# Keys and values of a fused transformer kernel: five evacuated blocks per sigmoid unit, value weights split in two loads, the down product's first operand tiles made before the values end

## The chip, the cores and the metric

The kernel runs as one launch on one core of a Trainium2 chip. The metric is device time in microseconds (us), lower is better. Before the change three runs took 1525.17 us in the median (1520.86 to 1525.78). The engines in this text: PE (TensorE, matmul), ACT (ScalarE), DVE (VectorE), POOL (GpSimd, which here issues loads and takes maxima over partitions), SP (SyncE, which here issues stores and loads).

## The reference

A model of two layers on 4096 tokens of width 256: cross-attention with mask, a feed-forward layer whose weights and activations are quantised, a second cross-attention with 16 heads of 64, and a mixture of 8 experts. The part around the change is the quantised layer and the projections of the second attention's keys and values:

```python
def act_qdq(x):
    scale = jnp.maximum(jnp.max(jnp.abs(x)) / qmax, 1e-12)      # one maximum over the whole tensor
    return jnp.clip(jnp.round(x / scale), -qmax - 1.0, qmax) * scale
...
up = act_qdq(x @ lpbq_dequant(w_up).T)
gate = act_qdq(x @ lpbq_dequant(w_gate).T)
sig = fixed_qdq_u16(jax.nn.sigmoid(gate))
gate = act_qdq(gate * sig)
o = act_qdq(gate * up)
return o @ lpbq_dequant(w_down).T
...
k = (key @ Wk + bk); v = (value @ Wv + bv)                       # of the second attention, key = value = ctx_1024
```

Every `act_qdq` needs the maximum of its whole input before the first element of its output can be made. There are three of them between the gate product and the down product; the kernel calls their scales GATE, SILU and INNER.

## The kernel before, in words

The stage around the change is one function (tiles named `b_...`). In it PE makes the up and the gate product. Then the elementwise chain of the quantised layer has to run on ACT and DVE, in which PE has no part; so PE meanwhile makes the keys and values of the second attention, whose input doesn't depend on this layer.

Keys and values are 128 blocks of 128x512 (64 of keys, then 64 of values), each of six matmuls (operands are split in a high and a low part, and three of the four products are made). A block needs a bank of PSUM; seven banks go round, so PE may be at most seven blocks ahead of the copies. ACT copies every block to one of five buffers (`outs`), and SP stores the buffer to HBM. Eight consecutive blocks share one part of the context, a "turn" of 1 MB: POOL loads its high and its low half (512 KB each) into one of two buffers, once the turn before the last is through.

The order on each engine is written out by hand.

- ACT: four copies, then twelve sigmoid units (`sigmoid(u)`: two instructions of 128x2048, L1145 and L1147), each followed by four copies, then three copies. Then it waits for the scale SILU and makes twelve quantised units (L1152), two ahead, and after each of the first ones 3, 3, 3 and 4 copies in turn. Then the rest of the copies; before the last eight, PE transposes the down weights into three banks, and ACT copies those too.
- DVE: per sigmoid unit a product (L1360), the quantising of the unit after the next (L1354) and a maximum (L1365). Then the scale SILU. Then per unit a product (L1380) and a maximum (L1383); in the last six units also two of the twelve steps that quantise the down weights each (L1313 to L1323). Then the scale INNER.
- POOL: one queue of loads and of `maximum(n)`, the step that turns DVE's 128 partial maxima into the one maximum (L911). `maximum(SILU)` stands before the loads of the values' first weights (1 MB, `load_half(WV, 0)`) and of turn 8, the first turn of the values. `maximum(INNER)` stands before the loads of the last two turns, 14 and 15.
- PE: block 64 (the first of the values) waits for turn 8 and the first weights, block 68 for the second half of the weights, block 112 for turn 14. After block 127 PE waits for the first tile of the down product's operand, which DVE rounds (L1438) and splits (L1446, with ACT's L1216 between) only after block 127 is done (`dve.wait_ge(block_done, ALL)`). After every two tiles of the down product come eight small matmuls (`idle_sums`, L1011), which wait for `b_w`, four loads of 128 KB that SP issues in `load_w2` (L849). SP issues the first of those after the last block is stored.

A count used below: "104 blocks done" means that PE has finished blocks 0 to 103.

Of the kernel before, what the change touches and what calls it, by code (L numbers as in the profile page):

```python
# [15 lines left out]
ALU = mybir.AluOpType  # L16
ACT = mybir.ActivationFunctionType
# [620 lines left out]
def feed_forward0(nc, ident, yT, ymax, upT, gateT, downT, w_gate, w_down, x1_dram, x2_dram, mv2, rstd2, b1T_dram, w2_dram,  # L638
# [16 lines left out]
    with ExitStack() as stack:  # L655
# [53 lines left out]
        down_int = x_space[:, 0:NF * D // 4].bitcast(I16)  # L709
# [60 lines left out]
        w_loaded, ctx_loaded = pool_loaded  # L770
# [25 lines left out]
        GROUPS = PIECES // 4  # L796
        TURN_FROM = ALL - 8
        IDLE_PIECES = 2 * FB
        WK, CONTEXT, WV = 0, 2, 2 + NC

        def bank(n):
# [11 lines left out]
        with nc.Block() as block:  # L813
# [79 lines left out]
            @block.gpsimd  # L893
            def _(pool):
                def load_half(k, h):
                    pool.dma_start(w_parts[:, h].rearrange("p a k n -> p a (k n)"), split_dram[k].bitcast(F32R)).then_inc(w_loaded[h], 16)

                def load_part(turn, a):
                    pool.dma_start(ctx_parts[turn % 2][a][:].rearrange("p k n -> p (k n)"), split_dram[CONTEXT + turn % NC][:, a, :].bitcast(F32R))\
                        .then_inc(ctx_loaded[turn % 2], 16)  # L900

                def load_contexts(first, end):
                    for turn in range(first, end):
                        if turn >= 2:
                            pool.wait_ge(block_done, BLOCKS * (turn - 1))
                        load_part(turn, 0)
                        load_part(turn, 1)

                def maximum(n):
                    pool.wait_ge(part_max, n + 1)  # L910
                    pool.partition_all_reduce(one[:, 1, :], one[:, 0, :], P, bass.bass_isa.ReduceOp.max).then_inc(all_max, 1)  # L911

                pool.memset(power[:], -0.5).then_inc(consts, 1)
                pool.wait_ge(consts, 1)
                pool.partition_all_reduce(one[:, 6, :], power[:, 0:1], P, bass.bass_isa.ReduceOp.max).then_inc(all_max, 1)
                for semaphore in finished:
                    pool.sem_clear(semaphore)
                maximum(UP)
                for s in range(2):
                    pool.wait_ge(split_stored[s], 16 * ITEMS // 2)  # L920
                load_part(0, 0)
                pool.wait_ge(y_ready, 2 * NC)
                load_half(WK, 0)
                load_half(WK + 1, 1)
                pool.wait_ge(product_done, (2 * NC - 1) * NF)
                load_part(0, 1)
                pool.wait_ge(product_done, 2 * NC * NF)
                load_contexts(1, 2)
# [12 lines left out]
                for n, (first, end) in enumerate(((0, NB - 2 * TILES), (NB - 2 * TILES, NB - TILES), (NB - TILES, NB))):  # L941
                    pool.wait_ge(mv_done, end)
                    part = slice(first, end)
                    pool.tensor_scalar(var2[:, part], mv2[:, part, 1], EPS, None, ALU.add).then_inc(var_done, 1)
                    pool.wait_ge(var_done, n + 1)
                    pool.tensor_tensor(rstd2[:, part], var2[:, part], power[:, part], ALU.pow).then_inc(rstd_done, 1)

            @block.tensor
            def _(pe):
# [90 lines left out]
                def value_block(n):  # L1040
                    c, rest = divmod(n - KEYS, BLOCKS)
                    h, t = divmod(rest, TILES)
                    if c == 0 and t == 0:
                        pe.wait_ge(w_loaded[h], 32)
                    for j, (k, (a, b)) in enumerate(product(range(ND), PARTS)):
                        last = pe.matmul(ps[:, bank(n), :], ctx_parts[c % 2][a][:, k, t * P:(t + 1) * P], w_parts[:, h, b, k, :],  # L1046
                                         start=(j == 0), stop=(j == ND * len(PARTS) - 1))
                    last.then_inc(block_done, 1)

                for n in range(ALL):  # L1050
# [8 lines left out]
                        key_block(n)  # L1059
                    else:  # L1060
                        value_block(n)
                pe.wait_ge(block_copied, ALL)
                pe.wait_ge(w_ready, 3)

                def down(c, s):
# [3 lines left out]
                    for t in range(TILES):  # L1069
# [2 lines left out]
                            pe.wait_ge(inner_ready, t + 1)  # L1072
                        if n >= TILES:
                            pe.wait_ge(x2_ready, n - TILES + 1)
                        for j, (f, (a, b)) in enumerate(product(range(NF), PARTS)):
# [12 lines left out]
            def _(act):  # L1088
# [124 lines left out]
                for t in range(TILES):  # L1213
                    act.wait_ge(inner_rounded, t + 1)
                    tok = slice(t * P, (t + 1) * P)
                    act.activation(inner[:, 0, 0, :, tok], inner16[:, 0, :, tok], ACT.Copy).then_inc(inner_high, 1)  # L1216
# [7 lines left out]
            def _(dve):  # L1224
# [175 lines left out]
                dve.wait_ge(max_done, 2 * NF * NC + 2 * NU)  # L1400
                then(dve.tensor_tensor(one[:, 5, :], factors[:, SILU, 0, :], factors[:, UP, 0, :], ALU.mult))
                scale_of(INNER, pmax[:, 0:NU], one[:, 5, :])
                rest_of_weights(2, downT, down_parts)
# [7 lines left out]
                def residual(t, s):  # L1411
                    dve.wait_ge(down_done, t + 1)
                    dve.wait_ge(x1_loaded[s], 16 * (t // 4 + 1 if isinstance(t, int) else turn[0] + 1))
                    if inside(t, 4, NB - 1):
                        dve.wait_ge(x2_stored[s], 16 * (t // 4 if isinstance(t, int) else turn[0]))
                    dve.scalar_tensor_tensor(x2_sb[:, s, :], ps[:, s, 0:D], factors[:, INNER, 0, :],
                                             x1_sb[:, s, :], ALU.mult, ALU.add).then_inc(x2_ready, 1)
                    dve.wait_ge(all_max, 1)
                    dve.wait_ge(x2_ready, t + 1)
# [13 lines left out]
                        residual(TILES * c + t, t)  # L1433


                for t in range(TILES):
                    tok = slice(t * P, (t + 1) * P)
                    dve.tensor_scalar(inner16[:, 0, :, tok], act_sb[:, :, tok], factors[:, INNER, 1, :], None, ALU.mult)\  # L1438
                       .then_inc(inner_rounded, 1)
                for t in range(TILES):  # L1440
                    if t == 2:
                        dve.tensor_scalar(inner16[:, 1], act_sb[:, :, CH:2 * CH], factors[:, INNER, 1, :], None, ALU.mult)\
                           .then_inc(inner_rounded, 1)
                    dve.wait_ge(inner_high, t + 1)
                    tok = slice(t * P, (t + 1) * P)
                    dve.tensor_tensor(inner[:, 0, 1, :, tok], inner16[:, 0, :, tok], inner[:, 0, 0, :, tok].bitcast(F32),  # L1446
                                      ALU.subtract).then_inc(inner_ready, 1)
# [1136 lines left out]
def cross_attention_network(nc, eye, x, ctx, ctx_blocks, ctx_t, mask_t, w_up, w_gate, w_down, w, experts_w, out):  # L2584
# [7 lines left out]
    with ExitStack() as persistent:  # L2592
# [13 lines left out]
        pool_loaded = [[persistent.enter_context(nc.semaphore(f"{name}_loaded{n}")) for n in range(2)] for name in ("w", "ctx")]  # L2606
        with ExitStack() as first:
            yT = sb(first, "yT", [P, ND, NB * P])

# [73 lines left out]
```

## Time and profile before

| | |
|---|---|
| median of 3 runs | 1525.17 us (1520.86 to 1525.78) |
| profiled execution, its own time | 1523.21 us |
| its span | 1521.4 us |
| busy share of the span | PE 89%, DVE 74%, ACT 69%, POOL 25% |
| granted TensorE clock, mean | 0.955 |
| bytes moved | 191.05 MB, mean 126 GB/s |
| keys and values | PE from about 445.1 us to 636.4 us |
| down product | PE from 639.7 us to 722 us |

The profiled execution took 1.8 us more than its span. Busy shares are means over stages with different limits; what bounds keys and values must be read from that stretch alone: where PE is idle in it, what ended each idle time, and at which clock PE went on.

### The profile page before, as it was taken

The page shows a single profiled execution, that of the slowest core. Times are in us where ns is not written, and L with a number is a line of the kernel's source. Part 1 is how long each engine was busy: PE and PEld are TensorE (multiplying, and loading weights), DVE is VectorE, ACT ScalarE, POOL GpSimd, SP SyncE. Part 2 cuts the span into 40 slices and gives each one's busy share as a digit, 9 for nine tenths or more (in the row PEclk, how much of TensorE's full clock was granted, in tenths as well). Part 3 has the DMA queues.
Part 4 walks back from the last instruction along what each step waited for, and adds up shares of the span by engine and source line. Part 5 has one row for each costly group of instructions (what it writes and reads, how often), then busy time and mean ns, then how long its engine had stood idle before and what let it go on. Part 6 is the DMA issues. An engine that isn't in the chain of part 4 may idle for free. (4 is left out here: it accounts for less than half of the span.)

```text
span 1521.4 us, 34563 instructions
## 1 busy us (share of the span) xinstructions
PE 1354.5 (89%) x11261; PEld 1154.8 (76%) x11261; DVE 1127.4 (74%) x1948; ACT 1046.9 (69%) x2716; POOL 374.4 (25%) x639
## 2 busy tenths in 40 slices
PE   5788888699899989999599999999999859999996
PEld 2455555487787768788488888888888649999996
DVE  6677777797859887266377777677777559888995
ACT  4677777666559976552477787777777428888885
POOL 5344444200001010002011111111111124445443
PEclk9999999899999999999799999999999859999999
DMA  7311011248038889766412332332331058111110
GB/s 222 123 36 31 28 32 34 89 153 303 28 125 253 265 283 301 261 206 198 177 64 78 129 102 87 121 102 78 129 112 60 29 198 311 64 55 50 51 46 10
DMA packets 102060, 191.05 MB, mean 126 GB/s; under 512 B 12948, under 2 KB 68145, under 8 KB 95540
## 3 DMA queue, kind: packets, MB, share of 16 engines
q1 hardware_dynamic: 91572, 155.80, 30.3%
q0 software_dynamic: 10176, 33.57, 7.5%
q8 instruction: 69, 1.13, 0.3%
q14 instruction: 51, 0.42, 0.1%
q10 hardware_dynamic: 192, 0.13, 0.0%
HBM read 124.17 MB, written 68.03 MB: 126 GB/s over the span
## 5 line engine op out<-in xcount | busy, mean ns | idle before, releaser
L2001 ACT ACTIVATE c_w_raw<-c_ps_score,c_neg_max 128x128 f32<-128x128 f32 x512 | 183.4, 388 | 51.5 <-DVE c_neg_max L1861 50.7
L2374 PE MATMUL d_ps_hT<-d_zT,d_w_tile 128*128 128x128 f32 x1248 | 148.7, 278 | 1.6 <-DVE d_zT L2481 1.6
L2374 PEld LDWEIGHTS d_ps_hT<-d_zT,d_w_tile 128*128 128x128 f32 x1248 | 145.6, 195 | 2.3 <-DVE d_zT L2481 2.3
L2387 PE MATMUL d_ps_y<-d_w_parts,d_hT 128*128 128x256 f32 x936 | 120.3, 284 | 1.8 <-DVE d_res L2512 1.8
L581 ACT ACTIVATE a_probT<-a_ps_probT 128x512 f32<-128x512 f32 x128 | 71.3, 623 | 70.0 <-PE a_ps_probT L368 69.9
L2547 ACT ACTIVATE d_h<-d_ps_hT,d_b1T 128x128 f32<-128x128 f32 x312 | 88.7, 367 | 41.3 <-PE d_ps_hT L2374 41.3
L459 DVE TENSOR_REDUCE a_row_max<-a_ps_score 128x8 f32<-128x1024 f32 x64 | 78.0, 1219 | 52.0 <-PE a_ps_score L357 52.0
L2001 ACT ACTIVATION_READ_ACCUMULATOR c_w_raw<-c_ps_score,c_neg_max 128x1 f32 x512 | 116.0, 227 | 0.0
L2387 PEld LDWEIGHTS d_ps_y<-d_w_parts,d_hT 128*128 128x128 f32 x936 | 113.2, 188 | 2.1 <-DVE d_res L2512 2.0
L1738 PE MATMUL c_ps_proj<-c_xnT,c_wq 128*128 128x256 f32 x768 | 108.6, 293 | 0.0
L2500 DVE TENSOR_TENSOR d_w_parts<-d_w,d_w_parts 128x1024 fp32r<-128x1024 f32 x78 | 95.3, 1222 | 10.9 <-ACT d_w_parts L2559 10.9
L1738 PEld LDWEIGHTS c_ps_proj<-c_xnT,c_wq 128*128 128x128 f32 x768 | 97.1, 195 | 5.0 <-issue 5.0
L1786 PE MATMUL c_ps_aux<-c_wo,c_attnT 128*128 128x256 f32 x768 | 100.4, 287 | 0.0
L1861 DVE TENSOR_REDUCE c_neg_max<-c_ps_score 128x4 f32<-128x512 f32 x128 | 82.5, 686 | 22.9 <-PE c_ps_score L1708 22.9
L1786 PEld LDWEIGHTS c_ps_aux<-c_wo,c_attnT 128*128 128x128 f32 x768 | 93.8, 189 | 4.3 <-issue 0.4
L1868 DVE TENSOR_TENSOR c_w_raw<-c_w_raw,c_inv_sum 128x512 f32<-128x512 f32 x128 | 88.9, 695 | 4.4
L1103 ACT ACTIVATE b_act<-b_ps 128x512 f32<-128x512 f32 (+1 forms) x96 | 54.9, 602 | 51.3 <-PE b_ps L988 44.1
L2559 ACT ACTIVATE d_w_parts<-d_w 128x1024 fp32r x78 | 82.0, 1052 | 10.0 <-PE d_ps_y L2387 10.0
L1046 PE MATMUL b_ps<-b_w_parts,b_ctx_high 128*128 128x512 f32 x256 | 82.0, 402 | 4.1 <-DMA b_ctx_low<-split_scratch 4.1
L1036 PE MATMUL b_ps<-b_ctx_high,b_w_parts 128*128 128x512 f32 x256 | 82.5, 397 | 2.9 <-ACT b_out L1161 2.8
L569 ACT ACTIVATE a_prob<-a_ps_score,a_shift 128x128 f32<-128x128 f32 x256 | 75.4, 413 | 11.5 <-DVE a_shift L463 10.2
L1683 POOL TENSOR_TENSOR c_var_o<-c_mv_o,c_eps 128x1 f32<-128x1 f32 x32 | 6.1, 192 | 303.3 <-DVE c_mv_o L1902 303.3
(302 smaller groups left out, 3538.3 us busy)
## 6 DMA issues: line engine op xcount, KB each, us to landing
keys_scratch<-b_out SPq DMA_DIRECT2D x64, 256.0 KB, 3.3
values_scratch<-b_out SPq DMA_DIRECT2D x64, 256.0 KB, 3.9
c_kT<-keys_scratch SPq DMA_DIRECT2D x16, 1024.0 KB, 6.3
d_w<-w_in SPq DMA_DIRECT2D x16, 1024.0 KB, 7.0
split_scratch<-b_split SPq DMA_DIRECT2D x12, 1024.0 KB, 4.7
c_v_more<-values_scratch SPq DMA_DIRECT2D x24, 512.0 KB, 4.0
b_ctx_high<-split_scratch POOLq DMA_DIRECT2D x16, 512.0 KB, 5.9
b_ctx_low<-split_scratch POOLq DMA_DIRECT2D x16, 512.0 KB, 6.4
```

What stands on the lines that cost most here:

```text
L1036: last = pe.matmul(ps[:, bank(n), :], w_parts[:, h, a, k, column:column + P], ctx_parts[c % 2][b][:, k, :], start=(j == 0), stop=(j == ND ...
L1046: last = pe.matmul(ps[:, bank(n), :], ctx_parts[c % 2][a][:, k, t * P:(t + 1) * P], w_parts[:, h, b, k, :], start=(j == 0), stop=(j == ND ...
L1738: last = pe.matmul(ps_proj[:, j, h * PT:(h + 1) * PT], weights[:, a, k, blk * P:(blk + 1) * P], src[:, c, k, :], start=(n == 0), stop=(n = ...
L1786: last = pe.matmul(ps_aux[:, 0:D], attnT[:, s, a, blk, :], wo[:, c, blk, :], start=False, stop=(n == BLKS * len(PARTS) - 1))
L1861: dve.tensor_reduce(neg_max[:, n, :], ps_score[:, n % 2], AX_X, ALU.max, negate=True).then_inc(max_done, 1)
L1868: dve.tensor_tensor(prob[:, n], prob[:, n], inv_sum[:, n, :].unsqueeze(2).to_broadcast([P, HB, P]), ALU.mult).then_inc(prob_ready, 1)
L2001: last = act.activation(prob[:, n, j, :], ps_score[:, n % 2, j, :], ACT.Exp, bias=neg_max[:, n, j:j + 1], accum_out=row_sum[:, n, j:j + 1])
L2374: last = pe.matmul(ps_hT[:, f, :], w1_tile[:, half, k, n * P:(n + 1) * P], zT[:, s, k, :], start=(k == 0), stop=(k == ND - 1))
L2387: last = pe.matmul(ps_y[:, 0:D], hT[:, s, a, f, :], w2_parts[:, half, b, n, :], start=(f == 0 and (a, b) == PARTS[0]), stop=(f == FB - 1 a ...
L2500: dve.tensor_tensor(w2_parts[:, half, 1], w2[:, e, half * FB // 2:(half + 1) * FB // 2, :], w2_parts[:, half, 0].bitcast(F32), ALU.subtrac ...
L2547: act.activation(h[:, f, :], ps_hT[:, f, :], ACT.Relu, bias=b1T[:, e, f:f + 1]).then_inc(h_ready, 1)
L2559: act.activation(w2_parts[:, half, 0], w2[:, e, half * FB // 2:(half + 1) * FB // 2, :], ACT.Copy)\
```

## The change

There are four edits.

1. ACT copies five blocks after a sigmoid unit, and four after every third one, in place of four throughout (56 against 48 in the twelve units). In the SILU stage it copies four after each unit.
2. The high part of the values' first weights gets a place of its own (`wv_high`, in `x_space`) and is loaded (512 KB) right after turn 1, ahead of `maximum(GATE)`. Where 1 MB was loaded, only the low part (512 KB) still is. The integers of the down weights move out of `x_space` for that.
3. The first two tiles of the down product's operand get a place of their own (`inner_first`); DVE rounds them right after the scale INNER, ACT makes their high parts between copies, DVE their low parts after those of the down weights. Two of the four tiles are still made after the last block.
4. The down product uses banks 3 to 6 in place of 0 to 3, and waits for the copy of the block that had the bank instead of for all copies.

```diff
@@ gpsimd
                 load_contexts(1, 2)
+                pool.dma_start(wv_high[:].rearrange("p k n -> p (k n)"), split_dram[WV][:, 0, :].bitcast(F32R)).then_inc(wv_high_loaded, 16)
                 maximum(GATE)
                 load_contexts(2, 8)
                 maximum(SILU)
                 pool.wait_ge(block_done, KEYS - 4)
-                load_half(WV, 0)
+                pool.dma_start(w_parts[:, 0, 1].rearrange("p k n -> p (k n)"), split_dram[WV][:, 1, :].bitcast(F32R)).then_inc(wv_low_loaded, 16)
                 load_contexts(8, 9)
@@ tensor
-                pe.wait_ge(block_copied, ALL)
                 pe.wait_ge(w_ready, 3)
...
+                        else:
+                            pe.wait_ge(block_copied, ALL - BANKS + 1 + t)
...
-                            last = pe.matmul(ps[:, t, 0:D], inner[:, s, a, f, t * P:(t + 1) * P],
+                            last = pe.matmul(ps[:, DOWN_BANK + t, 0:D], inner[:, s, a, f, t * P:(t + 1) * P],
@@ scalar
                 for u in range(NU):
                     sigmoid(u)
-                    copy_blocks(done, done + 4)
-                    done += 4
+                    more = 4 if u % 3 == 2 else 5
+                    copy_blocks(done, done + more)
+                    done += more
...
                 for u in range(NU):
-                    more = 4 if u % 4 == 3 else 3
-                    copy_blocks(done, done + more)
-                    done += more
+                    copy_blocks(done, done + 4)
+                    done += 4
                     if u + 2 < NU:
                         quantise_silu(u + 2)
...
-                copy_blocks(TURN_FROM + 2, ALL)
+                copy_blocks(TURN_FROM + 2, TURN_FROM + 4)
+                for t in range(FIRST_TILES):
+                    high_first(t, inner_first[:, :, t * P:(t + 1) * P])
+                copy_blocks(TURN_FROM + 4, ALL)
@@ vector
                     if (half, step) == (0, 0):
                         dve.wait_ge(down_loaded, 16)
+                        dve.wait_ge(block_done, KEYS - 4)
...
+                for t in range(FIRST_TILES):
+                    integers(t, inner_first[:, :, t * P:(t + 1) * P])
                 rest_of_weights(2, downT, down_parts)
+                for t in range(FIRST_TILES):
+                    low_first(t, inner_first[:, :, t * P:(t + 1) * P])
                 dve.wait_ge(block_done, ALL)
+                dve.wait_ge(inner_ready, FIRST_TILES)
```

On POOL, at the end of the key blocks, the queue stood so before (the ISA row is `maximum(SILU)`; behind it the values' first weights, turn 8, the second weights, turn 9):

```order
L899 DMA b_ctx_low_2916<-split_scratch 128x1024
L911 ISA b_one<-b_one 128x1
L896 DMA b_w_parts<-split_scratch 128x2048
L899 DMA b_ctx_high_2913<-split_scratch 128x1024
L899 DMA b_ctx_low_2914<-split_scratch 128x1024
```

and now so:

```order
L905 DMA b_ctx_low_2916<-split_scratch 128x1024
L917 ISA b_one<-b_one 128x1
L940 DMA b_w_parts<-split_scratch 128x1024
L905 DMA b_ctx_high_2913<-split_scratch 128x1024
L905 DMA b_ctx_low_2914<-split_scratch 128x1024
```

The first load behind the maximum is half as large; the maximum stands where it stood.

On ACT, in the SILU stage, the order from the last sigmoid unit's copies on was this before (`b_out` rows are copies of blocks, L1161 of keys, L1163 of values; `yT` rows are quantised units):

```order
L1161 ACTIVATE b_out_2923<-b_ps,b_bk 128x512
L1152 ACTIVATE yT<-b_act,b_factors 128x2048 x2
L1161 ACTIVATE b_out_2920<-b_ps,b_bk 128x512
L1161 ACTIVATE b_out_2921<-b_ps,b_bk 128x512
L1161 ACTIVATE b_out<-b_ps,b_bk 128x512
L1152 ACTIVATE yT<-b_act,b_factors 128x2048
L1161 ACTIVATE b_out_2922<-b_ps,b_bk 128x512
```

and is now this (L1174 keys, L1176 values):

```order
L1174 ACTIVATE b_out<-b_ps,b_bk 128x512
L1165 ACTIVATE yT<-b_act,b_factors 128x2048 x2
L1174 ACTIVATE b_out_2924<-b_ps,b_bk 128x512
L1176 ACTIVATE b_out_2925<-b_ps 128x512
L1176 ACTIVATE b_out_2922<-b_ps 128x512
L1176 ACTIVATE b_out_2923<-b_ps 128x512
L1165 ACTIVATE yT<-b_act,b_factors 128x2048
```

The copies before the first quantised unit are 63 where they were 55. The third quantised unit stood behind three key blocks; it stands behind the last key block and three value blocks.

## Rows read from the trace of the kernel before

**Rows 1.** What PE waited for, 440 to 645 us: total, times, longest.
```profile
PE b_ps L1046 <- DMA b_ctx_low<-split_scratch: 4.1, 1, 4.1
PE b_ps L1076 <- DVE b_inner L1446: 3.3, 1, 3.3
```

**Rows 2.** Stretches: us, busy PE PEld DVE ACT POOL (count), PEclk, DMA share, GB/s.
```profile
385.00:390.00 5.00, 4.87 (x15) 3.97 (x16) 5.00 (x7) 4.22 (x8) 0.00 (x0) 0.69 0.37 108
482.00:539.00 57.00, 54.11 (x225) 41.15 (x223) 50.12 (x31) 54.66 (x57) 7.13 (x10) 1.00 0.80 254
540.00:545.00 5.00, 1.80 (x4) 1.50 (x5) 4.96 (x3) 0.61 (x2) 1.01 (x2) 0.67 1.06 355
545.00:550.00 5.00, 5.00 (x16) 3.90 (x15) 4.93 (x3) 2.77 (x3) 0.00 (x0) 0.65 1.09 382
640.00:645.00 5.00, 5.00 (x32) 5.00 (x31) 3.90 (x5) 2.99 (x3) 0.00 (x0) 0.66 0.96 336
```

**Rows 3.** Timeline of ACT: start, length, line, what [idle before <-releaser].
```profile
478.16 2.02 ACT L1145 ACTIVATE b_act<-yT,b_factors 128x2048 f32<-128x2048 int16 x1
480.22 1.92 ACT L1147 ACTIVATE b_act<-b_act 128x2048 int32<-128x2048 f32 x1
482.04 2.40 ACT L1161 ACTIVATE b_out<-b_ps,b_bk 128x512 f32<-128x512 f32 x4
484.31 2.02 ACT L1145 ACTIVATE b_act<-yT,b_factors 128x2048 f32<-128x2048 int16 x1
...
525.11 4.40 ACT L1161 ACTIVATE b_out<-b_ps,b_bk 128x512 f32<-128x512 f32 x7
```

**Rows 4.** Timeline of POOL: the maxima and the loads of weights and turns.
```profile
530.34 0.35 POOL L911 PARTITION_ALL_REDUCE b_one<-b_one  x1 [13.14 <-DVE b_one L1239]
533.33 0.55 POOL L896 DMA_DIRECT2D b_w_parts<-split_scratch  x1 [2.64 <-PE b_ps L1036]
...
534.40 0.55 POOL L899 DMA_DIRECT2D b_ctx_low<-split_scratch  x1
...
598.41 0.35 POOL L911 PARTITION_ALL_REDUCE b_one<-b_one  x1 [6.59 <-DVE b_one L1239]
601.96 0.55 POOL L899 DMA_DIRECT2D b_ctx_high<-split_scratch  x1 [3.21 <-PE b_ps L1046]
...
613.06 0.53 POOL L899 DMA_DIRECT2D b_ctx_high<-split_scratch  x1 [10.02 <-PE b_ps L1046]
```

**Rows 5.** Timeline of PE: the first matmuls of the values and of the down product.
```profile
543.20 1.22 PE L1046 MATMUL b_ps<-b_w_parts,b_ctx_high 128*128 128x512 f32 x2 [4.08 <-DMA b_ctx_low<-split_scratch]
...
639.66 0.35 PE L1076 MATMUL b_ps<-b_down_high,b_inner 128*128 128x256 f32 x1 [3.26 <-DVE b_inner L1446]
...
645.61 0.64 PE L1011 MATMUL b_ps<-b_w,b_b1T 128*32 128x256 f32 x8
```

**Rows 6.** Loads issued at 534.40, at 446.11 and at 602.51 us: KB, us to landing.
```profile
b_ctx_low<-split_scratch POOLq DMA_DIRECT2D x1, 512.0 KB, 8.8
...
b_ctx_low<-split_scratch POOLq DMA_DIRECT2D x1, 512.0 KB, 5.2
...
b_ctx_low<-split_scratch POOLq DMA_DIRECT2D x1, 512.0 KB, 8.4
```

**Rows 7.** Timeline of DVE: units 6 and 11 of the SILU stage, the last step.
```profile
563.36 2.28 DVE L1380 TENSOR_TENSOR b_act<-yT,b_up 128x2048 f32<-128x2048 int16 x1
...
591.97 2.29 DVE L1380 TENSOR_TENSOR b_act<-yT,b_up 128x2048 f32<-128x2048 int16 x1
...
597.08 0.96 DVE L1323 TENSOR_TENSOR downT<-b_x_space,b_stats 128x768 f32<-128x768 int16 x1
```

**Rows 8.** What PE waited for over the whole span, one line: total, times, longest.
```profile
PE b_ps L988 <- ACT b_act L1103: 7.8, 1, 7.8
```

**Rows 9.** SP's issue of the first `b_w`, and loads from 639.7 to 641.7 us.
```profile
639.78 1.86 SPq L849 DMA_DIRECT2D b_w<-w_in  x4
...
b_w<-w_in SPq DMA_DIRECT2D x4, 128.0 KB, 3.3
```

More of the change, by code:

```diff
@@ L708, in feed_forward0 @@
         idle = out2[:].rearrange("p (g d) -> p g d", g=2)
-        down_int = x_space[:, 0:NF * D // 4].bitcast(I16)
+        wv_high = raw_at("wv_high", [P, ND, CH], address["x_space"], F32R)
+        down_int = spare[:, 0:NF * D // 4].bitcast(I16)
+        inner_first = raw_at("inner_first", [P, NF, 2 * P], address["yT"], I16)
         outs = [raw_at("out0", [P, CH], address["upT"] + 4 * ITEM), raw_at("out1", [P, CH], address["gateT"] + 4 * ITEM), out2,
@@ L769, in feed_forward0 @@
         down_copied = sem("down_copied")
-        w_loaded, ctx_loaded = pool_loaded
+        w_loaded, ctx_loaded, (wv_high_loaded, wv_low_loaded) = pool_loaded
         block_done = sem("block_done")
@@ L798, in feed_forward0 @@
         IDLE_PIECES = 2 * FB
+        DOWN_BANK = 3
+        FIRST_TILES = 2
+        assert (ALL - BANKS + 6 + 2) % BANKS == DOWN_BANK
         WK, CONTEXT, WV = 0, 2, 2 + NC
@@ L1043, in value_block @@
                     if c == 0 and t == 0:
-                        pe.wait_ge(w_loaded[h], 32)
+                        if h == 0:
+                            pe.wait_ge(wv_high_loaded, 16)
+                            pe.wait_ge(wv_low_loaded, 16)
+                        else:
+                            pe.wait_ge(w_loaded[h], 32)
+                    values = (wv_high if h == 0 else w_parts[:, 1, 0]), w_parts[:, h, 1]
                     for j, (k, (a, b)) in enumerate(product(range(ND), PARTS)):
-                        last = pe.matmul(ps[:, bank(n), :], ctx_parts[c % 2][a][:, k, t * P:(t + 1) * P], w_parts[:, h, b, k, :],
+                        last = pe.matmul(ps[:, bank(n), :], ctx_parts[c % 2][a][:, k, t * P:(t + 1) * P], values[b][:, k, :],
                                          start=(j == 0), stop=(j == ND * len(PARTS) - 1))
@@ L1074, in down @@
                             pe.wait_ge(x2_ready, n - TILES + 1)
+                        else:
+                            pe.wait_ge(block_copied, ALL - BANKS + 1 + t)
                         for j, (f, (a, b)) in enumerate(product(range(NF), PARTS)):
-                            last = pe.matmul(ps[:, t, 0:D], inner[:, s, a, f, t * P:(t + 1) * P],
+                            last = pe.matmul(ps[:, DOWN_BANK + t, 0:D], inner[:, s, a, f, t * P:(t + 1) * P],
                                              down_parts[b][:, f, :], start=(j == 0), stop=(j == NF * len(PARTS) - 1))
@@ L1200, in _, with high_first @@
                 round_weights(downT, down_parts)
-                copy_blocks(TURN_FROM + 2, ALL)
+                copy_blocks(TURN_FROM + 2, TURN_FROM + 4)
+                def high_first(t, src):
+                    act.wait_ge(inner_rounded, t + 1)
+                    act.activation(inner[:, 0, 0, :, t * P:(t + 1) * P], src, ACT.Copy).then_inc(inner_high, 1)
+                for t in range(FIRST_TILES):
+                    high_first(t, inner_first[:, :, t * P:(t + 1) * P])
+                copy_blocks(TURN_FROM + 4, ALL)
                 def high_inner(c, s):
@@ L1211, in high_inner @@
                     act.activation(inner[:, s, 0], inner16[:, s], ACT.Copy).then_inc(inner_high, 1)
[L1213 to L1216, printed above, removed]
+                for t in range(FIRST_TILES, TILES):
+                    high_first(t, inner16[:, 0, :, t * P:(t + 1) * P])
                 high_inner(1, 1)
@@ L1402, in _, with integers, low_first @@
                 scale_of(INNER, pmax[:, 0:NU], one[:, 5, :])
+                def integers(t, dst):
+                    dve.tensor_scalar(dst, act_sb[:, :, t * P:(t + 1) * P], factors[:, INNER, 1, :], None, ALU.mult).then_inc(inner_rounded, 1)
+                def low_first(t, src):
+                    dve.wait_ge(inner_high, t + 1)
+                    dve.tensor_tensor(inner[:, 0, 1, :, t * P:(t + 1) * P], src, inner[:, 0, 0, :, t * P:(t + 1) * P].bitcast(F32),
+                                      ALU.subtract).then_inc(inner_ready, 1)
+                for t in range(FIRST_TILES):
+                    integers(t, inner_first[:, :, t * P:(t + 1) * P])
                 rest_of_weights(2, downT, down_parts)
+                for t in range(FIRST_TILES):
+                    low_first(t, inner_first[:, :, t * P:(t + 1) * P])
                 dve.wait_ge(block_done, ALL)
+                dve.wait_ge(inner_ready, FIRST_TILES)
                 def low_inner(c, s):
@@ L1415, in residual @@
                         dve.wait_ge(x2_stored[s], 16 * (t // 4 if isinstance(t, int) else turn[0]))
-                    dve.scalar_tensor_tensor(x2_sb[:, s, :], ps[:, s, 0:D], factors[:, INNER, 0, :],
+                    dve.scalar_tensor_tensor(x2_sb[:, s, :], ps[:, DOWN_BANK + s, 0:D], factors[:, INNER, 0, :],
                                              x1_sb[:, s, :], ALU.mult, ALU.add).then_inc(x2_ready, 1)
@@ L1433, in chunk @@
                         residual(TILES * c + t, t)
[L1436 to L1447, printed above, removed]
+                for t in range(FIRST_TILES, TILES):
+                    integers(t, inner16[:, 0, :, t * P:(t + 1) * P])
+                low_first(2, inner16[:, 0, :, 2 * P:3 * P])
+                dve.tensor_scalar(inner16[:, 1], act_sb[:, :, CH:2 * CH], factors[:, INNER, 1, :], None, ALU.mult)\
+                   .then_inc(inner_rounded, 1)
+                low_first(3, inner16[:, 0, :, 3 * P:4 * P])
                 for c in range(2):
@@ L2604, in cross_attention_network @@
         ident_loaded = persistent.enter_context(nc.semaphore("ident_loaded"))
-        pool_loaded = [[persistent.enter_context(nc.semaphore(f"{name}_loaded{n}")) for n in range(2)] for name in ("w", "ctx")]
+        pool_loaded = [[persistent.enter_context(nc.semaphore(f"{name}_loaded{n}")) for n in range(2)] for name in ("w", "ctx", "wv")]
         with ExitStack() as first:
```

## The prediction, made before the changed kernel ran

> **What bounds the kernel now.** I read the waits of PE over keys and values first, then the windows for the clock, then the timelines of ACT, POOL and DVE with the landing times of the loads. PE is the engine that ends this stretch. It loses time in three places. (1) The key blocks: from 482 to 539 us PE is busy for 54.11 of 57 us at full clock [rows 2]; ACT needs 6.15 us for a sigmoid unit and four copies (478.16 to 484.31, [rows 3]), that is 1.54 us a block. PE's own pace is read from the loads that wait for it: 104 blocks done at 601.96, 112 at 613.06 [rows 4], so 11.1 / 8 = 1.39 us. (2) Block 64 waits 4.1 us for turn 8 [rows 1, 5], and then runs at the lower clock of 1.2 GHz: the mean clock of 0.65 and 0.67 [rows 2] costs (1 - 0.65) x 5 = 1.75 us from 545 to 550, and half of the 1.8 busy us before it, 0.9; 2.6 us in all. (3) The first down tile waits 3.3 us for its operand [rows 1, 5], and costs (1 - 0.66) x 5 = 1.7 us of clock behind it [rows 2]. DVE and ACT have room, but they make two maxima, and POOL's queue holds loads behind each.
>
> **Edit 1 in the key blocks.** A copy in a row of copies takes (484.31 - 482.04) / 4 = 0.57 us [rows 3]. Fourteen copies in three units then take 3 x 6.15 + 2 x 0.57 = 19.6 us, 1.40 each: ACT keeps PE's pace, and no bank is missed. PE, which starts the keys at 445.1, finishes block 63 at about 445.1 + 64 x 1.39 = 534.1 us, where it was 543.20 - 4.08 = 539.1 [rows 5]. That is the gain that the edit offers, 5.0 us.
>
> **But the maximum comes later.** Eight more copies stand ahead of the last sigmoid unit: 8 x 0.57 = 4.6 us on ACT. Its end was where the x7 copies begin, 525.11 [rows 3]; it becomes 529.7. DVE's product and maximum hang on it, so `maximum(SILU)`, which ended at 530.34 + 0.35 = 530.7 [rows 4], ends at 535.3. Before, POOL was through with it 2.6 us before the weights' load might go (60 blocks done, 533.33, [rows 4]). Now 60 blocks are done at 528.5, and POOL stands in the maximum until 535.3, with the low weights and turn 8 queued behind it. PE has been idle since 534.1 by then.
>
> **Edit 2, how long the loads take.** Before, 2 MB went from 533.33 to 534.40 + 8.8 = 543.2, 9.9 us, with key stores beside them. Bounds for the 1.5 MB now: 1 MB on quiet DMA engines took 0.53 + 5.2 = 5.7 us (446.11, [rows 6]), 2 MB on busy ones 9.9. I add half a MB at the 382 GB/s of rows 2, 1.4 us, to the quiet case, since few key stores are still under way then: 7.1 us. Block 64 starts at 535.3 + 7.1 = 542.4, against 543.2: 0.8 us gained, between 2.2 gained and 2.0 lost. So the early 512 KB and the 5.0 us of edit 1 pay for the later maximum and leave next to nothing. The clock after it: a wait of 7.8 us was followed by a mean clock of 0.69 over 5 us [rows 2, 8], 1.5 us lost; one of 4.1 us by 2.6 lost. I take 2.1, a gain of 0.5. Loading the high weights early costs POOL 0.5 us ahead of `maximum(GATE)`, hidden, since ACT is then still copying its first four blocks.
>
> The Trainium skill, "DMA: Bandwidth & Descriptors", section Bandwidth, gives 6.15 us for a load of 1 MB and 341 GB/s, and under "Issuing engines are not separate DMA queues" it says that transfers of all engines share the same 16 engines and interleave. By its rate 1.5 MB would be an estimate of about 6.15 x 1.5 = 9.2 us, block 64 at 544.5 and the sum 2.1 us longer; the 5.7 us for 1 MB in this trace speak for the shorter time, the 9.9 beside stores agree with the interleaving.
>
> **Edit 1 in the SILU stage.** Each quantised unit now stands behind four copies, and four blocks take PE 5.6 us, where DVE alone needs 4.5 per unit. The chain that was bound by DVE is now bound by PE. The last unit (11) stands behind the copy of block 102. 104 blocks are done at 601.96 - 0.8 = 601.2 (I leave the clock's 0.5 out), 103 at 599.8; with the copy, 0.6, and the unit, 2.0, DVE can begin unit 11 at 602.4. Counted over DVE it is the same: unit 6 is quantised at about 573.9, and units 6 to 11 took 591.97 - 563.36 = 28.6 us, 602.5. Then 598.04 - 591.97 = 6.1 us to the end of the last step [rows 7], and 0.8 to the end of `maximum(INNER)`, whose rows end at 598.76 [rows 4]: 609.3. Before it was through 3.2 us ahead of its turn; now turn 14, which could be loaded from 601.2 on, is loaded from 609.3. Bounds for its 1 MB: 5.7 us quiet, (602.51 + 8.4) - 601.96 = 8.95 us beside value stores [rows 4, 6]. The stores fade once PE stands still; I take 7.4, landing at 616.7. PE needs it when 112 blocks are done, 613.06 - 0.8 = 612.2. A new wait of 4.5 us (2.8 to 6.1), and clock behind it of 2.0 us (1.5 to 2.6, as above): together 6.5 us lost. Turn 15 follows with nothing in its way. The down weights' steps and the scale INNER are 10 us later, with 20 us to spare before the weights are transposed.
>
> **Edits 3 and 4.** Call X the end of block 127 (636.4 before). The first two tiles are ready before X (rounded at about 610, split behind the down weights), and PE starts at X, not X + 3.3. Two tiles take 4.3 us at full clock (36 matmuls of 0.12). Then the small matmuls need `b_w`: SP issues it at 639.78 to 641.64, the last of four at about 641.2, landing 3.3 us later [rows 9]: 644.5, X + 8.1. SP hangs on X as before. So PE waits 3.7 us there instead. Tile 2 starts at X + 8.1 + 0.6 = X + 8.7, against X + 9.8 before (645.61 + 0.6, [rows 5]): 1.1 us gained, in which the old loss of clock is already counted. The new wait should bring a loss of the same kind, 1.4 (0 to 2.6): 0.3 us lost, between 1.1 gained and 1.5 lost.
>
> **The sum.** -0.8 - 0.5 + 6.5 + 0.3 = +5.5 us. On the profiled execution's 1523.2 us that is 1528.7; that execution lies 2.0 us below the median of the runs, from which it is 1530.7. I predict 1530 us. What a measurement of this kernel can tell from no change is 0.3%, 4.6 us, so the line between "same" and "slower" is 1529.7, and that to "faster" 1520.6.
>
> **The rivals.** (A) Turn 14 lands in time: POOL takes the INNER maximum by 604 or so. For it: only if ACT runs ahead with its units, which its order forbids while each unit stands behind four copies. If DVE's weight steps hide elsewhere and the load takes 5.7 us, the wait is nearly 3 us shorter, not gone. Time: -0.8 - 0.5 + 0.3 = -1.0, 1522 to 1524. Chance 0.25, for the length of a chain that I extrapolate over 60 us. (B) Faster: the values start when the keys end. Place: POOL at the SILU maximum. If sigmoid units pass at the old 6.15 us with five copies in them, the maximum ends at 530.7, the loads run from there and land at 537.8: 5.4 us earlier, and a wait of 3.4 us, whose clock costs 1.7 and not 2.6 us. With the SILU stage ahead by as much and turn 14 in time the sum is -5.4 - 0.9 + 0.3 = -6.0, 1517 to 1519. It decides from a maximum that ends before 532. Against it: ACT is busy for 54.66 of 57 us [rows 2] and can't hide 4.6. Chance 0.12. (C) Slower still: at 1.39 us a block the key stores and turns ask for more than the 254 GB/s of rows 2, stores land late, ACT waits for its five buffers in the sigmoid stage and the SILU maximum slips by 2 more us; loads take the upper bounds, 9.9 and 8.95. Then +2.0 + 1.0 in place of -0.8, 6.1 + 2.6 in place of 6.5, and +1.5: about +12, 1535 to 1537. Chance 0.13. The forecast keeps 0.50, with its own range 1526.5 to 1534, seven tenths of it above the line.
>
> **How the numbers follow.** Slower: 0.13 + 0.35 = 0.48. Same: 0.25 + 0.13 of the forecast's lower part = 0.38. Faster: 0.12, and 0.02 of the forecast and A together: 0.14. The range is 1519 to 1536: it takes in the forecast, A, the upper edge of B and most of C.
>
> **What would show it.** Right: ACT's period per three sigmoid units near 19.6 us, no PE idle before 534; POOL's SILU maximum near 535; one PE idle of 7 to 9 us before the first value block at 541 to 545; POOL's INNER maximum near 609 and PE idle for 3 to 6 us before block 112, ended by the load of `b_ctx_low`; the first down tile right behind block 127, then an idle of 3 to 4 us ahead of L1011, ended by `b_w`. Wrong: value blocks that start before 540, or a PE without a break from there to block 127.

## The result, and where the profile after shows the time

The changed kernel takes 1541.48 us in the median of 7 runs, against 1525.42 us of the kernel before, measured beside it; the ratio is 1.0102, with a 95% interval of 1.0083 to 1.0122. That is 13 to 19 us slower. The prediction was 1530 us, with a range up to 1536: the direction came out, the time lies above the range. The profiled execution of the changed kernel took 1537.05 us, 4.4 us less than the median, so the stretches below show less than the whole 16 us.

Three stretches can be compared. The keys start where POOL issues the loads of turn 1, which wait for the last gate product; the next attention starts with PE's first matmul on `c_xn`. Of the kernel before (POOL and PE timelines: start, length, line, what, [idle before <-releaser]):

```profile
445.58 0.53 POOL L899 DMA_DIRECT2D b_ctx_high<-split_scratch  x1 [7.84 <-PE b_ps L988]
...
731.43 0.69 PE L1770 MATMUL c_ps_aux<-ident,c_xn 128*128 128x128 f32 x2 [8.99 <-DVE c_xn L1856]
```

and of the changed kernel:

```profile
444.43 0.53 POOL L905 DMA_DIRECT2D b_ctx_high<-split_scratch  x1 [7.87 <-PE b_ps L995]
...
741.60 0.69 PE L1798 MATMUL c_ps_aux<-ident,c_xn 128*128 128x128 f32 x2 [9.17 <-DVE c_xn L1884]
```

Between them lie 285.9 us before and 297.2 us after, 11.3 us more. The part in front (445.6 and 444.4) holds none of the change, nor does the part behind, 1521.4 - 731.4 = 790.0 and 1535.3 - 741.6 = 793.7. The times below count from the start of the keys where two kernels are compared. What PE waited for from 430 to 660 us in the changed kernel (total, times, longest):

```profile
PE b_ps L1058 <- DMA b_ctx_low<-split_scratch: 17.8, 2, 11.1
PE b_ps L1018 <- DMA b_w<-w_in: 3.8, 1, 3.8
PE b_ps L1043 <- ACT b_out L1174: 1.1, 1, 1.1
```

One wait of 4.1 us on a turn [rows 1] has become two, of 11.1 and 6.7 us. The 3.3 us before the down product have become 3.8 us before the first small matmuls. The key blocks themselves are faster. The third row is PE waiting for a bank that ACT has yet to copy, 1.1 us in one wait. In the kernel before it was

```profile
PE b_ps L1036 <- ACT b_out L1161: 2.8, 8, 0.4
```

PE is through with the keys 90.2 us behind their start (545.72 - 11.10 - 444.43), against 93.5 before (543.20 - 4.08 - 445.58): 3.3 us gained. PE's rows at the three waits, which answer to [rows 5]:

```profile
545.72 0.80 PE L1058 MATMUL b_ps<-b_wv_high,b_ctx_high 128*128 128x512 f32 x1 [11.10 <-DMA b_ctx_low<-split_scratch]
...
620.75 0.80 PE L1058 MATMUL b_ps<-b_wv_high,b_ctx_high 128*128 128x512 f32 x1 [6.69 <-DMA b_ctx_low<-split_scratch]
...
654.11 0.64 PE L1018 MATMUL b_ps<-b_w,b_b1T 128*32 128x256 f32 x8 [3.82 <-DMA b_w<-w_in]
```

POOL's timeline says who was late, as [rows 4] do for before:

```profile
537.28 0.34 POOL L917 PARTITION_ALL_REDUCE b_one<-b_one  x1 [24.97 <-DVE b_one L1258]
537.49 0.55 POOL L940 DMA_DIRECT2D b_w_parts<-split_scratch  x1
...
611.55 0.34 POOL L917 PARTITION_ALL_REDUCE b_one<-b_one  x1 [18.01 <-DVE b_one L1258]
611.77 0.55 POOL L905 DMA_DIRECT2D b_ctx_high<-split_scratch  x1
...
614.37 0.53 POOL L905 DMA_DIRECT2D b_ctx_high<-split_scratch  x1 [1.52 <-PE b_ps L1058]
```

POOL stands idle for 25 us and for 18 us, both times until DVE hands it the partial maxima, and each load goes at once behind the maximum. Before, the load behind the SILU maximum waited for PE's blocks (2.64 us, [rows 4]), and so did the one behind the INNER maximum (3.21 us). At 614.37, when 112 blocks are done, turn 14 is still on its way. The SILU maximum ends 93.2 us after the keys start, against 85.1 before: 8.1 us later. ACT's timeline shows why it is not the 4.6 us of eight copies:

```profile
482.82 1.25 ACT L1174 ACTIVATE b_out<-b_ps,b_bk 128x512 f32<-128x512 f32 x2
485.43 2.07 ACT L1174 ACTIVATE b_out<-b_ps,b_bk 128x512 f32<-128x512 f32 x3 [1.36 <-DMA keys_scratch<-b_out]
...
519.33 2.24 ACT L1174 ACTIVATE b_out<-b_ps,b_bk 128x512 f32<-128x512 f32 x3 [1.09 <-DMA keys_scratch<-b_out]
...
532.05 4.39 ACT L1174 ACTIVATE b_out<-b_ps,b_bk 128x512 f32<-128x512 f32 x7
```

Groups of five copies break after the second: the buffer of the third still waits for its store to land.

The clock behind the waits (stretches of 5 us; PEclk is 0.62 in the first row and 0.61 in the second), as in [rows 2]:

```profile
545.00:550.00 5.00, 4.28 (x12) 3.42 (x13) 4.69 (x3) 0.60 (x1) 0.00 (x0) 0.62 1.08 398
620.00:625.00 5.00, 4.25 (x12) 3.40 (x13) 0.00 (x0) 0.60 (x1) 0.00 (x0) 0.61 0.53 192
```

Both times PE goes on at 1.2 GHz for about 3 us and loses about 1.5 us, no more behind 11.1 us of idling than behind 6.7. (The mean of 0.62 makes 1.9 us over the 5 us, of which half of the 0.72 us in which PE was still idle doesn't count.)

### The profile page after: what moved, and what is told of

Same layout as the page of the kernel before. It is cut to its first block and busy times, and to the rows that moved or that the text cites. A ratio compares the mean times of both kernels' runs of the same rounds, so it can differ in the third digit from the quotient of the medians.

```text
span 1535.3 us, 34569 instructions
## 1 busy us (share of the span) xinstructions
PE 1358.5 (88%) x11261; PEld 1160.7 (76%) x11261; DVE 1129.6 (74%) x1948; ACT 1047.2 (68%) x2716; POOL 374.3 (24%) x640
## 5 line engine op out<-in xcount | busy, mean ns | idle before, releaser
L569 ACT ACTIVATE a_prob<-a_ps_score,a_shift 128x128 f32<-128x128 f32 x256 | 75.0, 409 | 12.2 <-DVE a_shift L463 11.3
L1736 PE MATMUL c_ps_score<-c_kT,c_qT 64*128 64x128 f32 x1024 | 76.8, 291 | 5.0 <-issue 3.4
```

## The experiments

Two theories stood against each other. The first: the loads of the next stage stand in POOL's queue behind a maximum that comes late. The second: at the faster pace of the key blocks the DMA engines are the limit, and the loads would be late wherever they stood. Seven of the twelve runs move loads, three take parts of the change, one has a sixth buffer, and one is the changed kernel again. "Stretch" is the time from the start of the keys to the next attention in the profiled execution. The ratio is to the kernel before, measured beside each group of runs, where its median was 1524.8 to 1526.3 us; medians of different rows are less comparable than ratios. The one kernel that was profiled twice, the changed one, shows stretches 2.8 us apart, so a difference of 3 us or less between two single profiles is a hint and no more.

| kernel | median us | ratio (95%) | stretch us |
|---|---|---|---|
| before | 1525.4 | | 285.9 |
| changed | 1541.5 | 1.0102 (1.0083 to 1.0122) | 297.2 |
| changed, again | 1540.7 | 1.0097 (1.0074 to 1.0121) | 300.0 |
| SILU maximum moved | 1531.5 | 1.0050 (1.0031 to 1.0069) | 289.4 |
| INNER maximum moved | 1529.6 | 1.0032 (1.0015 to 1.0049) | 292.5 |
| both moved | 1522.7 | 0.9978 (0.9960 to 0.9995) | 284.7 |
| both, `b_w` ahead | 1520.7 | 0.9969 (0.9952 to 0.9987) | 279.6 |
| and turn 8 first | 1518.3 | 0.9953 (0.9934 to 0.9973) | 279.1 |
| and second weights ahead | 1518.0 | 0.9941 (0.9919 to 0.9964) | 276.7 |
| before, sigmoid counts | 1533.6 | 1.0056 (1.0033 to 1.0079) | 290.7 |
| the same, six buffers | 1526.6 | 1.0005 (0.9989 to 1.0020) | 287.7 |
| before, all counts | 1539.2 | 1.0089 (1.0060 to 1.0117) | 299.2 |
| changed, old counts | 1523.0 | 0.9997 (0.9973 to 1.0021) | 283.1 |
| before, POOL's order | 1524.2 | 0.9983 (0.9970 to 0.9997) | 285.9 |

**The SILU maximum behind the loads.**

```diff
-                maximum(SILU)
                 pool.wait_ge(block_done, KEYS - 4)
                 pool.dma_start(w_parts[:, 0, 1] ...).then_inc(wv_low_loaded, 16)
                 load_contexts(8, 9)
+                maximum(SILU)
```

> The changed kernel, with POOL's SILU maximum moved behind the loads of the values' low weights and of turn 8. Theory (the maxima of the elementwise chain stand ahead of the loads in POOL's queue): the loads go when 60 blocks are done, 84 us after the keys start, and land about 8 us later, so the 11.1 us wait before block 64 shrinks to 1 to 3 us; the INNER maximum stays where it is, and since DVE then bounds the SILU stage it comes at most 8 us earlier, so a wait before block 112 of 5 to 8 us stays. 6 to 9 us faster than the changed kernel, still about 7 us slower than the kernel before. Rival (the DMA engines are the limit at the faster pace of the key blocks): the loads land as late as before against block 64, 4 us of wait or more remain, and the stores to HBM hold ACT instead; within 3 us of the changed kernel.

PE's waits from 430 to 670 us in that kernel:

```profile
PE b_ps L1058 <- DMA b_ctx_low<-split_scratch: 10.6, 2, 6.8
```

The 11.1 us are down to 3.8, a little more than the 1 to 3 expected, the 6.8 us before block 112 stay, and the ratio falls from 1.0102 to 1.0050, by about 8 us. The median is 10.0 us lower and the stretch 7.8; expected were 6 to 9.

**The INNER maximum behind the loads.**

```diff
-                load_contexts(9, 14)
+                load_contexts(9, 16)
                 maximum(INNER)
-                load_contexts(14, 16)
```

> The changed kernel, with POOL's INNER maximum moved behind the loads of turns 14 and 15. Theory of the maxima: the 6.7 us wait before block 112 goes, with about 1.6 us of lower clock behind it; the 11.1 us wait before block 64 stays. 7 to 9 us faster than the changed kernel, about 7 us slower than before. The scale INNER comes when 112 blocks are done, still 20 us ahead of its use. Rival (DMA engines the limit): turn 14 lands late all the same, 3 us of wait or more remain.

```profile
PE b_ps L1057 <- DMA b_ctx_low<-split_scratch: 11.5, 1, 11.5
```

Here the other wait goes and the first stays. The median falls by 11.9 us (11 by the ratios), above the expected 7 to 9, the stretch by 4.7 to 7.5, depending on which of the two profiles of the changed kernel it is held against.

**Both.** This is the two diffs together.

> The changed kernel, with both maxima moved behind the loads. Theory of the maxima: both waits go down to 1 to 3 us together, and both losses of clock with them; 16 to 19 us faster than the changed kernel, 3 to 7 us faster than the kernel before (5 us of key blocks, 2 us of the wait of block 64 and its 2.6 us of clock, less what is left). Rival (DMA engines the limit): less than 10 us faster than the changed kernel, slower than the kernel before.

```profile
PE b_ps L1017 <- DMA b_w<-w_in: 5.0, 1, 5.0
PE b_ps L1057 <- DMA b_ctx_low<-split_scratch: 4.1, 1, 4.1
```

18.8 us faster than the changed kernel, and 2 to 3 us faster than the kernel before, at the low end of what was expected, since 4.1 us of wait before block 64 are left: the order in POOL's queue accounts for the whole loss. As its main cause the DMA engines are refuted: the same bytes at the same pace of the key blocks cost one wait of 4.1 us, and the kernel is not slower than the one before. A smaller part they do have: the same 1.5 MB, issued when 60 blocks are done, let the first value block start 9.4 us later here (530.28 to 539.65) and 9.0 with the SILU maximum alone moved, where the changed kernel with the old counts of copies, below, needs 7.8 (531.82 to 539.57).

**Single edits.** The sigmoid counts alone, on the kernel before:

```diff
                     sigmoid(u)
-                    copy_blocks(done, done + 4)
-                    done += 4
+                    more = 4 if u % 3 == 2 else 5
+                    copy_blocks(done, done + more)
+                    done += more
```

> The kernel before, with five, five and four copies after the sigmoid units and nothing else of the change. Theory (maxima ahead of the loads): the SILU maximum ends about 93 us after the keys start instead of 85, 2 MB of loads go behind it and take 10 us, block 64 starts about 5.5 us later than before; the SILU stage keeps its three or four copies a unit, so the INNER maximum comes just in time for turn 14, no wait of 3 us or more before block 112. 5 to 8 us slower than the kernel before. Rival (the gain of the key blocks is real and the loads don't matter): 3 to 5 us faster than before.

and with the SILU stage's `copy_blocks(done, done + 4)` too:

> The kernel before, with all counts of copies changed (sigmoid and SILU stage) and nothing else of the change. Theory: the same late start of the values, and besides the INNER maximum comes behind the time at which turn 14 could be loaded, a wait of 5 to 8 us before block 112 and 1.6 us of lower clock. 12 to 16 us slower than the kernel before, that is 6 to 9 us slower than with the sigmoid counts alone. Rival: the SILU counts cost nothing, no more than 2 us slower than with the sigmoid counts alone.

PE's waits of the first (its L1046 are the values), then of the second:

```profile
PE b_ps L1046 <- DMA b_ctx_low<-split_scratch: 11.4, 1, 11.4
```

```profile
PE b_ps L1046 <- DMA b_ctx_low<-split_scratch: 17.5, 2, 11.5
```

Each set of counts makes its wait, 11.4 us by the sigmoid counts and 6.0 us more by the SILU counts. Block 64 starts 3.9 us later than before, where 5.5 were expected, for the 2 MB take 8.6 us (535.82 to 544.44) and not 10. In the stretch the first costs 4.9 us and both together 13.3. Medians say 8 and 14; intervals of 0.5% can't place them better.

What is left of the change is edits 2 to 4, the changed kernel with the old counts (4 in the sigmoid stage; 3, 3, 3, 4 in the SILU stage):

> The changed kernel with the old counts of copies in both stages, so the split load of the value weights and the first tiles alone. Theory: the loads go as before, when 60 blocks are done, and 512 KB less of them land 1.5 to 2.5 us earlier, so the wait before block 64 is 1.5 to 2.5 us instead of 4.1; no wait before block 112; the first down tile comes 3.3 us earlier and PE then waits 3.8 us for b_w. 0 to 5 us faster than the kernel before. Rival (one of these edits costs by itself, by the longer queue on POOL or by the move of the integers): slower than the kernel before by 2 us or more.

```profile
PE b_ps L1018 <- DMA b_w<-w_in: 3.8, 1, 3.8
PE b_ps L1043 <- ACT b_out L1174: 2.9, 9, 0.4
PE b_ps L1058 <- DMA b_ctx_low<-split_scratch: 2.0, 1, 2.0
```

With the split load the wait before block 64 is halved, and the first tiles trade 3.3 us of waiting for 3.8 us elsewhere. The stretch is 2.8 us shorter; the ratio of 0.9997 and one profile can't tell it from nothing. These edits cost nothing measurable.

**Why the maximum slipped by 8.1 us.** A sixth buffer, in a free part of `x_space`, on the kernel with the sigmoid counts alone:

```diff
-                raw_at("out3", ...), raw_at("out4", ...)]
+                raw_at("out3", ...), raw_at("out4", ...),
+                raw_at("out5", [P, CH], address["x_space"] + 4 * (NF * D // 4))]
```

> The kernel before with five, five and four copies after the sigmoid units (as in the run with the sigmoid counts alone), and six buffers for evacuated blocks instead of five. Theory (3.4 of the 8.1 us by which the SILU maximum slipped are ACT's waits for stores of keys): ACT's waits for key stores go, the SILU maximum ends about 88 to 90 us after the keys start instead of 92.7, block 64 starts 3 us earlier than with five buffers, so 2 to 4 us faster than that run. Rival (the slip comes from elsewhere, DVE or the units themselves): ACT's waits go, but the maximum stays within 1 us of 92.7.

With five buffers ACT waited for key stores in that stage, and the maximum came so (ACT's waits, POOL's timeline):

```profile
ACT b_out L1161 <- DMA keys_scratch<-b_out: 2.9, 3, 1.3
```

```profile
535.60 0.34 POOL L911 PARTITION_ALL_REDUCE b_one<-b_one  x1 [24.99 <-DVE b_one L1240]
```

With six buffers that kind of wait is gone from ACT's list, and

```profile
534.30 0.34 POOL L912 PARTITION_ALL_REDUCE b_one<-b_one  x1 [20.98 <-DVE b_one L1241]
```

With the start of the keys at 442.94 and 445.04 us the maximum ends 93.0 us behind it with five buffers and 89.6 with six. Before it was 85.1. So 3.4 us of the slip are waits for stores, and the 4.5 that are left fit the eight copies, as predicted. By the ratios (1.0056 and 1.0005) six buffers remove most of the cost of the sigmoid counts, by the stretch 3.0 of 4.9 us. PE's wait before block 64 hardly shrinks all the same:

```profile
PE b_ps L1047 <- DMA b_ctx_low<-split_scratch: 10.9, 1, 10.9
```

Block 64 starts 2.1 us earlier, at 99.4 us where it was 101.5, and not the 3 us expected, since the 2 MB now take 9.9 us instead of 8.6; and the keys end 1.6 us earlier too, at 88.5 us. Against the kernel before that is the whole 5.0 us that edit 1 was meant to gain; with five buffers it is 3.3.

**The changed kernel again.**

> The changed kernel itself once more, for the spread of stretches outside the change. Theory: the 3.7 us that the profile of the changed kernel shows beyond the down product belong to that execution and not to the change; a second profile shows 297 us (within 2) from the start of the keys to the start of the next attention, and 789 to 796 us behind it. Rival: the part behind is again 3 us or more above the 790.0 us of the kernel before, and the placement of data or stores costs there.

The stretch is 300.0 us this time, against 297.2, just outside what was expected, and the part behind it 792.1 us, against 793.7. Over all fourteen profiled executions that part lies between 789.8 and 796.1 us, whichever kernel it is; the one of before, 790.0, is near the lower end. Of the 16 us of the median the stretch explains 11 to 14.

**What is late next.** `b_w` ahead, on top of both maxima moved: its first buffer becomes turn 14's place, free when 120 blocks are done (the lines that swap the two places and leave out the old issue are not shown).

```diff
                 for n in range(ALL):
+                    if n == ALL - BLOCKS + 2:
+                        sp.wait_ge(block_done, ALL - BLOCKS)
+                        load_w2(0)
                     store_block(n)
```

> The kernel with both maxima moved, and besides the first four loads of b_w taken ahead: its buffer is the place of turn 14's high part, free when 120 blocks are done, and SP issues them between the stores of blocks 121 and 122. Theory (edit 3 only moved PE's wait from the first down tile to b_w): the 3.8 us wait before the first small matmuls goes, and the lower clock behind it, 1.7 us; 4 to 6 us faster than the kernel with both maxima moved, 8 to 12 us faster than the kernel before. Rival: the third down tile, whose operand is made after the last block, is late next, and at most 2 us are won.

```profile
PE b_ps L1060 <- DMA b_ctx_low<-split_scratch: 3.8, 1, 3.8
PE b_ps L1020 <- DMA b_w<-w_in: 2.1, 1, 2.1
PE b_ps L1091 <- DVE b_x_space L1452: 1.1, 1, 1.1
```

The stretch gains 5.1 us, as expected, the median only 2.1, which its scatter doesn't tell from 4. Against the kernel before it is 4 to 5 us faster (2 to 7 by the interval), and not the 8 to 12 expected. The 5.0 us of waiting turn into 1.1 us for the residual (the sum that frees a bank for the fifth down tile) and 2.1 us for the third `b_w`, ahead of the third group of small matmuls. Then turn 8 ahead of the low weights:

```diff
+                load_contexts(8, 9)
                 pool.wait_ge(block_done, KEYS - 4)
                 pool.dma_start(w_parts[:, 0, 1] ...).then_inc(wv_low_loaded, 16)
-                load_contexts(8, 9)
                 maximum(SILU)
```

> The kernel with both maxima moved and b_w ahead, and besides turn 8 loaded before the values' low weights, so that it goes when 56 blocks are done instead of 60. Theory: the wait of 3.8 us before block 64 shrinks to 2 us or less (512 KB behind 60 blocks done take 5 to 6 us against the 5.6 us of four blocks), and most of the lower clock behind it goes. 3 to 6 us faster than without this edit, 8 to 11 us faster than the kernel before. Rival: the earlier turn collides with the key stores, ACT waits for its buffers, and nothing is won.

```profile
PE b_ps L1060 <- DMA b_w_parts<-split_scratch: 3.4, 1, 3.4
```

The wait before block 64 is gone, but 0.5 us of the stretch and 2.4 us of the median are all that is won, where 3 to 6 were expected: a wait of 3.4 us has come up before block 68, whose weights POOL holds behind the SILU maximum. A miss by the very mechanism of this study. So these go ahead of the maximum too (`load_half(WV + 1, 1)` before `maximum(SILU)`):

> The best kernel so far (both maxima moved, b_w ahead, turn 8 first), and besides the values' second weights ahead of the SILU maximum too. Theory: they go when 64 blocks are done, 2.3 us earlier, so of the 3.4 us that block 68 now waits for them 1 to 1.5 us are left, and little of the lower clock behind it; 2 to 4 us faster between the start of the keys and the start of the next attention. Rival: the load competes with turn 9 and the key stores and lands no earlier.

```profile
PE b_ps L1060 <- DMA b_w_parts<-split_scratch: 2.1, 1, 2.1
```

The wait shrinks to 2.1 us, where 1 to 1.5 were expected. The stretch falls by 2.3 us; the median falls by 0.3 and the ratio by 0.0012, neither clear of noise. This kernel has the lowest median of the study: 1518.0 us, a ratio of 0.9941, 8 to 9 us faster than the kernel before; the runs can't tell it from the kernel with turn 8 first.

**POOL's order alone, on the kernel before.** Turn 8 before `maximum(SILU)`, and `maximum(INNER)` behind turn 15, nothing else.

> The kernel before with its counts of copies as they were, and only POOL's order changed: turn 8 ahead of the values' first weights, both maxima behind the loads. Theory: the wait of 4.1 us before block 64 goes down to 1 us or less, since turn 8 goes when 56 blocks are done and 1 MB of weights takes 5.1 us against the 5.6 us of four blocks; with the 2.6 us of lower clock, 4 to 7 us faster than the kernel before. Rival: four blocks are too short for the weights' 1 MB beside turn 8, PE waits 3 us or more, and at most 2 us are won.

```profile
PE b_ps L1045 <- DMA b_w_parts<-split_scratch: 2.3, 1, 2.3
```

2.3 us of wait stay, now for the 1 MB of weights, and a ratio of 0.9983 is 2 to 3 us won (0.5 to 4.6 by the interval) in the place of 4 to 7. The stretch shows none of it, 285.9 as before, though block 64 starts 1.7 us earlier. The weights don't land within four blocks: PE starts on them 8.1 us after their issue (533.82 to 541.87), where 5.1 were expected. The SILU maximum still stands ahead of the weights here, but it ends before they may go, so it delays nothing.

## Why the prediction was right and wrong

- **"But the maximum comes later": the mechanism right, the term too small.** The text made the slip 8 x 0.57 = 4.6 us; it was 8.1. The failed step is that ACT was timed as if its five buffers were always free. Rival C named that cause with 2 us and a chance of 0.13; the six buffers show 3.4 us. It also cut the gain of the key blocks, 3.3 us where 5.0 stood, but no term of the sum hangs on that.
- **"How long the loads take": too short.** I took 7.1 us for 1.5 MB; from 537.49 to 545.72 are 8.2. In the same place behind the late maximum the whole 2 MB took 8.6 us (the sigmoid counts alone), so edit 2 won only 0.4 us there. Together with the slip this puts block 64 at 101.3 us behind the start of the keys, against 97.6 before: 3.7 us later, where 0.8 us earlier stood in the sum. The clock gave 1.1 to 1.2 us back, more than the 0.5 forecast: 112 blocks are done 169.9 us behind the start, against 167.5.
- **"Edit 1 in the SILU stage": right, too small.** A new wait before block 112 of 6.7 us (5.6 in the second profile), forecast 4.5, with 1.5 us of clock. The INNER maximum ended 167.5 us behind the start of the keys, forecast 163.7, but PE was late by nearly as much (112 blocks done at 169.9, forecast 166.6). The mis-sized term is the load: I took 7.4 us for turn 14, and from 611.77 to PE's start at 620.75 are 9.0, the upper bound. Between 112 and 128 blocks done the change loses 8.2 us against 6.5.
- **"Edits 3 and 4": right.** PE starts the down product at once and waits 3.8 us for `b_w` (forecast 3.7). Net loss from the end of block 127 on 0.6 us, forecast 0.3.
- **The sum.** Forecast +5.5. Measured in the stretch 2.5 + 8.2 + 0.6 = +11.3. Of the 5.8 us between them 3.5 are the maximum's slip beyond the forecast (it ended at 93.2 us, forecast 89.7). The rest of the median's 16 us, 2 to 5 us, isn't in the changed stretch of these profiles, and stays open: the part behind it scatters by 6 us, which is as large.
- **Rival A** (turn 14 in time) and **rival B** (values start when the keys end) fell as argued. Rival C's account is the nearest to what happened: waits for buffers, the second load at its upper bound (9.0 us; the first took 8.2, not 9.9), and a sum of about +12 against the measured 11.3. Its time of 1535 to 1537 holds the profiled execution's 1537.05 and is 5 us short of the median. The forecast costed each term apart, and the slip and both loads came out too short. That one cause, fuller DMA engines, moved them together is argued and not shown.

## What to carry to other kernels

A queue that holds both loads and a step of a compute chain makes each load as late as that chain. When work is added on the engine that feeds the chain, look at what stands behind it in the other queues, and move the loads ahead before the work is added. When an engine is sped up to the pace of another one, its waits for free buffers must be costed anew: with no slack left, every late store goes into the chain. An operand that is made early only helps up to the next operand that is late; look for that one first.

## What the runs showed that was not expected

- The lower clock behind a wait cost no more after 11.1 us of idling (0.62 over 5 us) than after 6.7 (0.61); behind the 4.1 us of before it cost more, about 2.6 us [rows 2].
- 512 KB loaded first behind the maximum took 5.6 us to land, and each 512 KB more came only 1.3 us later:

```profile
b_w_parts<-split_scratch POOLq DMA_DIRECT2D x1, 512.0 KB, 5.6
...
b_ctx_low<-split_scratch POOLq DMA_DIRECT2D x1, 512.0 KB, 7.1
```

  (issued at 537.49 and at 538.55 us, so they land at 543.1 and 545.7). By that spacing, halving the first load would be worth 1.3 us, an estimate. Two pairs of runs give other values: 0.4 us in this place (8.6 and 8.2, above), and 2.1 us with the old counts, where 9.9 us [rows 4, 6] became 7.8. What a load costs here hangs on what else is under way.
